# Splitting the operands of a point-wise product, with the low parts of h on VectorE between box sums

## What is computed

```python
x = x + L0(gn(x))   # expert weights mixed by a sparsemax gate, then a 1x1 convolution
x = x + L1(gn(x))   # depthwise 3x3, batch norm, relu, prune; 1x1 convolution, batch norm, relu, prune
x = x + L2(gn(x))   # attention over the 784 pixels with squared, normalised queries and keys
x = x + L3(gn(x))   # 3x3 mean per channel
```

```python
amax = jnp.max(jnp.abs(h), axis=(2, 3), keepdims=True)
h = jnp.where(amax < 4.0, 0, h)                   # whole channels are set to zero
h = conv_general_dilated(h, pw_w, (1, 1), ...)    # the point-wise product, 256 x 256
```

## Time and profile before

| | before |
|---|---|
| median of 3 runs | 1625.71 us (1625.15 to 1627.07) |
| the profiled execution | 1624.92 us, its span 1623.1 us |
| TensorE busy | 1530.0 us, 94% of the span |
| VectorE busy | 1376.0 us, 85% |
| ScalarE busy | 1362.3 us, 84% |
| GpSimd busy | 189.1 us, 12% |
| mean granted TensorE clock | 0.973 of full speed |

### The profile page before, as it was taken

How to read it: one execution, slowest core, us unless ns; L and a number is a source line. 1 busy time by engine, 2 the same in 40 slices (tenths; PEclk the granted TensorE clock), 3 DMA queues, 4 the chain that set the end, 5 groups by cost and what they waited for, 6 DMA issues and landing times. The chain is left out here.

```text
span 1623.1 us, 26428 instructions
## 1 busy us (share of the span) xinstructions
PE 1530.0 (94%) x8190; PEld 1149.4 (71%) x8190; DVE 1376.0 (85%) x2466; ACT 1362.3 (84%) x3496; POOL 189.1 (12%) x142
## 2 busy tenths in 40 slices
PE   4469999999999999999999999999999999999993
PEld 2247777777777777777777777777777777776773
DVE  5877689999888998988889998888999988888446
ACT  3368998988999888899998889999888899987862
POOL 1111011011110101111011111101101111010000
PEclk8689999999999999999999999999999999999996
DMA  4000011000111110011111001111100011000001
GB/s 148 20 20 21 21 40 41 31 29 22 40 40 40 40 40 20 20 40 40 40 40 40 20 20 40 40 40 40 40 27 28 24 40 40 21 21 21 21 20 40
DMA packets 21058, 55.58 MB, mean 34 GB/s; under 512 B 2321, under 2 KB 3345, under 8 KB 21010
## 3 DMA queue, kind: packets, MB, share of 16 engines
q1 hardware_dynamic: 20914, 54.98, 9.6%
q10 hardware_dynamic: 96, 0.00, 0.0%
HBM read 29.29 MB, written 25.69 MB: 34 GB/s over the span
## 5 line engine op out<-in xcount | busy, mean ns | idle before, releaser
L770 DVE SCALAR_TENSOR_TENSOR h<-xpad,dw_sb,h 128x784 f32<-128x784 f32 x512 | 495.9, 1031 | 0.0
L541 PE MATMUL tile_ps<-wqk,xn_parts 128*112 128x512 f32 x1344 | 363.8, 425 | 0.0
L541 PEld LDWEIGHTS tile_ps<-wqk,xn_parts 128*112 128x112 f32 x1344 | 235.3, 175 | 79.6
L583 PE MATMUL tile_ps<-k,xT 112*128 112x256 f32 x896 | 205.2, 388 | 7.7 <-ACT xT L1026 7.7
L583 PEld LDWEIGHTS tile_ps<-k,xT 112*128 112x128 f32 x896 | 174.3, 195 | 40.2 <-issue 8.4
L449 PE MATMUL conv_ps<-h,pw_masked 128*128 128x392 f32 x512 | 180.5, 496 | 5.5 <-issue 5.5
L960 ACT ACTIVATE junk<-x 128x784 bf16<-128x784 f32 x192 | 162.3, 848 | 23.6 <-DVE x L797 15.5
L571 PE MATMUL conv_ps<-x,mixed 128*128 128x392 f32 (+1 forms) x512 | 175.1, 494 | 2.2 <-ACT mixed L994 1.1
L1234 POOL TENSOR_SCALAR pw_masked<-pw_sb,hmask 128x256 f32<-128x256 f32 x64 | 119.1, 1869 | 433.9 <-DVE hmask L778 425.5
L1221 POOL TENSOR_SCALAR xpad<-x,gn_r,gn_s 128x784 f32<-128x784 f32 x64 | 64.4, 1013 | 894.2 <-DVE gn_s L701 894.2
L449 PE MATMUL conv_ps<-xn_parts,w_out 128*128 128x392 f32 x768 | 152.7, 347 | 0.0
(11 more groups left out here) (138 smaller groups left out, 2646.9 us busy)
## 6 DMA issues: line engine op xcount, KB each, us to landing
x<-x SPq DMA_DIRECT2D x32, 784.0 KB, 4.3
out<-x SPq DMA_DIRECT2D x32, 784.0 KB, 3.4
expert_sb<-expert_rows SPq DMA_DIRECT2D x8, 256.0 KB, 5.2
x<-w_qk SPq DMA_DIRECT2D x1, 512.0 KB
x<-w_vT SPq DMA_DIRECT2D x1, 256.0 KB
x<-w_ln SPq DMA_DIRECT2D x1, 256.0 KB
pw_sb<-pw_wT SPq DMA_DIRECT2D x1, 256.0 KB
gmean<-group_mean SPq DMA_DIRECT2D x1, 64.0 KB, 3.8
```

The costliest lines, as they stand in the source:

```text
L541: mm = nc.tensor.matmul(bank, xn2_parts[:, u, i, m * TOK:(m + 1) * TOK], wqk[:, v, i, :], start=False, stop=(i == J - 1 and u == 1))
L583: mm = nc.tensor.matmul(tile_ps[:, KX_BANK, i * C:(i + 1) * C], xT[:, m, half(i)], k2[:, m, :], start=(m == 0), stop=(m == M - 1))
L770: ins = nc.vector.scalar_tensor_tensor(acc, view, scalar, acc, ALU.mult, ALU.add)
```

## The change

The mask is no longer put on the weights but on h, and the product is made of split operands.

- Setup: `pw_parts`, the high and low part of the point-wise weights, is made by VectorE from the loaded weights (a cast and a subtraction, 512 elements each). `mask_weights` is removed.
- GpSimd, `h_high`: for each half, h * mask over 784 elements, written in float32r.
- VectorE, `h_low`: for each half, h * mask - high, over 784 elements. `h_mask` is now two instructions, one for each half, the first of them bound to the first half's sum alone.
- VectorE's order: both masks, box sum 0, low part of half 0, box sum 1, low part of half 1, box sums 2 and 3, `reciprocal_sums`, seven taps, three taps. The reciprocals were behind the seven taps before.
- TensorE: a half of the point-wise product is 12 matmuls on split operands (8 instructions before), and waits for both low parts.
- To make room, `over` has one buffer for all sums and `junk` is shorter, with waits on ScalarE's own earlier instructions.

```diff
             def pointwise(C_, halves):
-                pe.wait_ge(h_ready.sem, h_ready.at(C_))
-                pe.wait_ge(pw_masked_ready.sem, pw_masked_ready.at(C_))
+                pe.wait_ge(h_lo.sem, h_lo.at(C_))
...
-                    conv_tile(j, [(pw_masked[:, i, :], h[:, C_.odd, i, :]) for i in range(J)]).then_inc(pw_mm.sem, 1)
+                    conv_tile(j, by_parts(pw_parts, h_parts)).then_inc(pw_mm.sem, 1)
...
+                parts_of(pw_parts, pw_raw)
                 parts_of(wqk, wqk_raw)
...
+            def h_mask(C_, j):
+
+                dve.wait_ge(h_over_sum.sem, h_over_sum.at(C_, j + 1))
                 if (C_ - 1).active:
+                    dve.wait_ge(h_hi.sem, h_hi.at(C_ - 1))
+                nc.vector.scalar_tensor_tensor(hmask[:, j:j + 1], h_over[:, j:j + 1], ones[:, 0:1], zeros[:], ALU.mult,
+                                               ALU.is_gt).then_inc(hmask_step.sem, 1)
+
+            def h_low(C_, j):
+
+                dve.wait_ge(h_hi.sem, h_hi.at(C_, j + 1))
+                if (C_ - 1).active:
+                    dve.wait_ge(pw_mm.sem, pw_mm.at(C_ - 1))
+                nc.vector.scalar_tensor_tensor(h_parts[:, 1, j, :], h[:, C_.odd, j, :], hmask[:, j:j + 1],
+                                               h_parts[:, 0, j, :].bitcast(F32), ALU.mult,
+                                               ALU.subtract).then_inc(h_lo.sem, 1)
...
                 if C_.active:
-                    h_mask(C_)
+                    h_mask(C_, 0)
+                    h_mask(C_, 1)
                 if F.active:
-                    box_sums(F, range(BOX_STEPS))
+                    box_sums(F, range(1))
+                if C_.active:
+                    h_low(C_, 0)
+                if F.active:
+                    box_sums(F, range(1, 2))
+                if C_.active:
+                    h_low(C_, 1)
+                if F.active:
+                    box_sums(F, range(2, BOX_STEPS))
+                if D.active:
+                    reciprocal_sums(D)
                 if B.active:
                     depthwise(B, slice(3, 10))
-                if D.active:
-                    reciprocal_sums(D)
...
-            def mask_weights(C_):
+            def h_high(C_, j):
 
                 if (C_ - 1).active:
                     pool.wait_ge(pw_mm.sem, pw_mm.at(C_ - 1))
-                pool.wait_ge(w_loaded, LOADED)
-                pool.wait_ge(hmask_step.sem, hmask_step.at(C_))
+                pool.wait_ge(hmask_step.sem, hmask_step.at(C_, j + 1))
                 hold(pool, "pool")
-                for j in range(J):
-                    nc.gpsimd.tensor_scalar(pw_masked[:, j, :], pw_sb[:, j, :], hmask[:, j:j + 1], 0.0, ALU.mult,
-                                            ALU.add).then_inc(pw_masked_ready.sem, 1)
+                nc.gpsimd.tensor_scalar(h_parts[:, 0, j, :], h[:, C_.odd, j, :], hmask[:, j:j + 1], 0.0, ALU.mult,
+                                        ALU.add).then_inc(h_hi.sem, 1)
```

More of the change, by code:

```diff
@@ L131, in build @@
         bn1_sb, bn2_sb = params[:, 4:8, :], params[:, 8:12, :]
-        pw_sb = sb("pw_sb", [P, J, C])
+        pw_parts = sb("pw_parts", [P, 2, J, C], F32R)
         wqk = sb("wqk", [P, 2, J, 2 * C], F32R)
@@ L155, in build @@
         h = sb("h", [P, 2, J, HW])
-        pw_masked = sb("pw_masked", [P, J, C])
+        h_parts = sb("h_parts", [P, 2, J, HW], F32R)
         x2 = sb("x2", [P, 2, J, HW])
@@ L162, in build @@
         k4 = sb("k4", [TOK, M, C])
-        junk = sb("junk", [P, M * C], BF16)
+        junk = sb("junk", [P, J * HW], BF16)
         xT = sb("xT", [TOK, M, C])
@@ L175, in build @@
         wvT_sb, wln_sb = wv_ln[:, 0], wv_ln[:, 1]
+        pw_raw = x3[:, 0].rearrange("p j n -> p (j n)")[:, J * 2 * C:J * 3 * C].rearrange("p (j n) -> p j n", j=J)
         bias_rows = xn2[0:1].rearrange("p j n -> p (j n)")[:, 0:3 * 2 * C].rearrange("p (k n) -> p k n", k=3)
@@ L197, in build @@
         below = sb("below", [P, 2])
-        over = sb("over", [P, 2, J, HW], BF16)
+        over = sb("over", [P, HW], BF16)
         h_over = sb("h_over", [P, J])
@@ L252, in build @@
         h_over_sum = sig("h_over_sum", J)
-        hmask_step = sig("hmask_step")
-        pw_masked_ready = sig("pw_masked_ready", J)
+        hmask_step = sig("hmask_step", J)
+        h_hi = sig("h_hi", J)
+        h_lo = sig("h_lo", J)
         pw_mm = sig("pw_mm", J)
@@ L353, in build @@
             (idn[:], ident),
-            (pw_sb[:], pw_wT.rearrange("(j p) o -> p j o", p=P)),
+            (pw_raw, pw_wT.rearrange("(j p) o -> p j o", p=P)),
         ]
@@ L760, in depthwise @@
                         if (B - 2).active:
-                            dve.wait_ge(pw_mm.sem, pw_mm.at(B - 2))
+                            dve.wait_ge(h_lo.sem, h_lo.at(B - 2))
                     acc = h[:, B.odd, j, :].rearrange("p (h w) -> p h w", w=W)
@@ L771, in depthwise @@
                     ins.then_inc(dw_step[j].sem, 1)
-            def h_mask(C_):
-                dve.wait_ge(h_over_sum.sem, h_over_sum.at(C_))
+            def h_mask(C_, j):
+                dve.wait_ge(h_over_sum.sem, h_over_sum.at(C_, j + 1))
                 if (C_ - 1).active:
-                    dve.wait_ge(pw_masked_ready.sem, pw_masked_ready.at(C_ - 1))
-                nc.vector.tensor_scalar(hmask[:], h_over[:], 0.0, None, ALU.is_gt).then_inc(hmask_step.sem, 1)
+                    dve.wait_ge(h_hi.sem, h_hi.at(C_ - 1))
[8 more added lines that the diff above has]
+                                               ALU.subtract).then_inc(h_lo.sem, 1)
             def make_x2(C_):
@@ L1069, in sum_over_h @@
                     act.wait_ge(hmask_step.sem, hmask_step.at(B - 1))
-                    act.wait_ge(h_over_sum.sem, h_over_sum.at(B - 1, j + 1))
+                    act.wait_ge(y_over_sum.sem, y_over_sum.at(B - 1))
+                if j:
+                    act.wait_ge(h_over_sum.sem, h_over_sum.at(B, j))
                 act.wait_ge(h_ready.sem, h_ready.at(B, j + 1))
-                nc.scalar.activation(over[:, 0, j, :], h[:, B.odd, j, :], ACT.Relu, bias=below[:, 0:1],
+                nc.scalar.activation(over[:], h[:, B.odd, j, :], ACT.Relu, bias=below[:, 0:1],
                                      accum_out=h_over[:, j:j + 1]).then_inc(h_over_sum.sem, 1)
@@ L1078, in sum_over_y @@
                     act.wait_ge(ymask_step.sem, ymask_step.at(C_ - 1))
-                    act.wait_ge(y_over_sum.sem, y_over_sum.at(C_ - 1, j + 1))
+                act.wait_ge(h_over_sum.sem, h_over_sum.at(C_))
+                if j:
+                    act.wait_ge(y_over_sum.sem, y_over_sum.at(C_, j))
                 act.wait_ge(y_ready.sem, y_ready.at(C_, j + 1))
-                nc.scalar.activation(over[:, 1, j, :], x2[:, C_.odd, j, :], ACT.Relu, bias=below[:, 1:2],
+                nc.scalar.activation(over[:], x2[:, C_.odd, j, :], ACT.Relu, bias=below[:, 1:2],
                                      accum_out=y_over[:, j:j + 1]).then_inc(y_over_sum.sem, 1)
@@ L1109, in q_norms @@
                 for m in range(M):
-                    nc.scalar.activation(junk[0:TOK, m * C:(m + 1) * C], q2[:, m, :], ACT.Square,
+                    slot = m % (J * HW // C)
+                    if slot < m:
+                        act.wait_ge(q4_ready.sem, q4_ready.at(D, slot + 1))
+                    nc.scalar.activation(junk[0:TOK, slot * C:(slot + 1) * C], q2[:, m, :], ACT.Square,
                                          scale=qk_rec[:, 0, m:m + 1],
@@ L1241, in step @@
                 if C_.active:
-                    mask_weights(C_)
+                    for j in range(J):
+                        h_high(C_, j)
             run(pool, step)
@@ L1249 @@
 SETUP_BN = SETUP_PARTS + 2
-SETUP_DVE = SETUP_BN + 10 + 2 + 2 + 2
+SETUP_DVE = SETUP_BN + 10 + 2 + 2 + 2 + 2
 SETUP_POOL = 10
```

## The result

The changed kernel takes 1642.08 us (median of 4 runs, 1641.64 to 1643.64) against 1625.86 us before (4 runs, 1625.15 to 1627.07): 1.0101 times the time, 95% interval 1.0088 to 1.0114. It is slower, by about what the prediction said (1640 us). The profiled execution, the longest of the four, took 1643.64 us, its span 1641.8 us.

A forecast was written before the change was run, and what follows sets the result against it. A loop through VectorE, as long as TensorE's, was taken as the bound: step 46.98 + 2.75 - 1.67 - 0.48 = 47.58 us. 1624.92 + 16.2 (27 steps) - 1.6 (ends) = 1639.5, said as 1640 us, range 1624 to 1662.

The forecast's parts named there:

- The shift of the taps, 2.75: On VectorE, the seven taps with the reciprocals ahead of them start 2.75 us later in each step.
- order (b): Box sum 0 runs ahead of GpSimd's first high part; stalls cost VectorE 1.55 us per step; the order taken.
- (a): GpSimd's first high part runs ahead of box sum 0; stalls cost VectorE 1.23 us per step.
- The wait for q_norm: VectorE's wait for q_norm, behind the taps, vanishes: 1.67 us off each step.
- The one for the square root: VectorE's wait for ScalarE's gn_sd shrinks from 0.78 us, taking 0.48 us off each step.
- a rival with a chance of 0.05: TensorE's clock drops behind its 1.6 us wait, 1.76 us per step: 1687 us; chance 0.05.
- the chain that the prediction called fixed: Work from kx_low through attention to the last square of k keeps a fixed distance, 24 us, and absorbs nothing.
- The ends, -1.6: Outside the 27 steps: setup +1.2 us, last two steps and keys_x wait -2.8, together -1.6.
- Full lock: Rival: each high part stops VectorE for 0.99 us, +1.06 us per step: 1652 us; chance 0.12.
- GpSimd slower in the rounded format: Rival: high parts at twice xpad's time give 1693 us, at a third more 1657; chance 0.09.
- Gain and loss cancel: Rival: fixed waits give 0.6 us or reciprocals start by 822.6: 1622 to 1629 us; chance 0.10.
- TensorE alone: Rival: TensorE is the only bound, so each step falls by its 0.8 us: 1603 us; chance 0.14.

The follow-up runs named there:

- experiment 7: Changed kernel with high and low parts on 16 of 784 columns and the reciprocals behind the seven taps, product incomplete: 1617.6 us, ratio 0.9946.
- experiment 4: Changed kernel with the point-wise product in plain float32 of the high parts only, low parts made but not multiplied: 1640.2 us, ratio 1.0091.
- experiment 2: Changed kernel with GpSimd's high parts on 16 of 784 columns, product incomplete: 1646.34 us, ratio 1.0135.
- experiment 9: Changed kernel with only the reciprocals moved behind two of the seven taps, masks late as in the change: 1644.23 us, ratio 1.0107.
- experiment 1: Changed kernel with the reciprocals moved back behind the seven taps: 1733.53 us, ratio 1.0671.
- 8: Changed kernel with the second sum over h and both masks early, reciprocals ahead of all seven taps: 1642.6 us, ratio 1.0106.
- 3: Changed kernel with high parts on 16 columns and the reciprocals behind two of the seven taps, product incomplete: 1602.83 us, ratio 0.986.
- 5: Changed kernel, computing everything, with the second sum over h and both masks early and the reciprocals behind two taps: 1594.71 us, ratio 0.981.
- 6: Kernel before the change with its sum over h and mask early: 1612.03 us, ratio 0.9915.

## Why the prediction was right

**Which loop bounds.** The prediction read from 0.2 us of waiting at kx_parts that a path through VectorE was as long as TensorE's. Shown: experiment 7 gives TensorE 0.9 us and gets 0.23; experiment 4 takes most of its saving back (0.6 us) and the ordinary step stays.

**The shift of the taps, 2.75.** Measured, in the step shown, 24.96 us from kx_low to the reciprocals against 22.29 to the seven taps before (820.44 less the kx_low at 798.15): 2.67. The kx_low of that step:

```profile
798.15 0.69 DVE L879 TENSOR_TENSOR kx_parts<-tile_ps,kx_parts 128x512 fp32r<-128x512 f32 x1 [0.16 <-ACT kx_parts L1127]
```

The prediction had it as the larger of two numbers that lie close together, 2.69 by k and 2.47 to 2.78 by VectorE's own work; both halves are now shown, by experiments 2 and 9. So the size of the stalls hardly mattered here: with none at all the step is the same (experiment 2), and the 2.75 would have come out nearly right with a wrong price. The price had errors. I took order (b), box sum 0 ahead of the first high part. It was (a): the high part started at 871.29, ahead of the second mask. Its price was 1.32, between the 1.23 of (a) and the 1.55 of (b), but it was paid by other instructions than I named: the second mask, for which I had put nothing, pays 0.65, and h_low(0) 0.67. With this price the sum would be 1.54 - 0.31 + 1.32 = 2.55. Most of the last 0.12 lies in the low parts themselves: one between two box sums adds 1.70 + 0.95 - 1.82 = 0.83, where 0.77 was said. How much of it is the wait for k is not separated; experiment 9, where nothing waits for k, is 0.07 shorter.

**What goes behind it.** The wait for q_norm vanished whole, 1.67. The one for the square root went from 0.78 to 0.27, where 0.30 was said. The row of the kernel before:

```profile
844.67 0.20 DVE L699 RECIPROCAL gn_r<-gn_sd 128x8 f32<-128x8 f32 x1 [0.78 <-ACT gn_sd L954]
```

From the step at 798.15 (47.08 us long; 46.98 is the mean of 27) this gives 47.08 + 2.67 - 1.67 - 0.51 = 47.57. Measured 47.47. The last 0.10 is in VectorE's busy time behind the reciprocals and I did not trace it further. Over 27 steps it makes 13.4 us where 16.2 were said.

**The clock.** Here the prediction's own case had nothing, and a rival with a chance of 0.05 had 1.76 us in every step. Neither is what happened: 5 of 27 steps lose 1.6 us, 8.1 in all. This is the largest error of the sum. In such a step the attention weights come late; VectorE in order of time, the low parts of the attention weights:

```profile
813.45 0.88 DVE L858 SCALAR_TENSOR_TENSOR attn_parts<-tile_ps,k_inv,attn_parts 128x256 fp32r<-128x256 f32 x2 [1.88 <-ACT attn_parts L1071]
```

The wait is 1.88 us instead of 0.3, on the chain that the prediction called fixed. Set beside TensorE's rest in an ordinary step, the runs are: 3.4 us in experiment 1 (the granted clock falls in 24 of 27 steps), 0.94 in the change and in experiments 2, 8 and 9 (4 to 6 long steps), 0.5 to 0.6 in 7 and 0.35 in 4 (none), under 0.1 in 3, 5 and 6 (none). Only experiment 4 against the change varies this rest with all other work kept. Why one step in five or six and not each stays open. TensorE's rest was forecast at 1.6 us at kx_parts; it is 0.94 as the trace counts it, most of it one stop earlier at k_norm, and 1.40 against the 46.07 us that TensorE needs when it never waits (experiment 5; forecast 46.0).

**The ends, -1.6.** Measured -2.8: the setup is later by 0.66 at the first kx_low (1.2 forecast), the first step is shorter by 0.81 (not forecast), the last part by 2.66 (2.8 forecast).

Together: 27 steps 2.8 too high, the clock 8.1 too low, the ends 1.2 too high, and the profiled execution took 1643.64 us instead of 1639.5. The mechanism of the ordinary step is the predicted one; that the total came so close is in part luck, for errors of 4 us to one side took half of the 8.1 us to the other away. Of the signs named beforehand three did not come: the wait at kx_parts is 0.4 us and not 1.4 to 1.8, TensorE's busy share of an ordinary step is 98% (46.53 of 47.47) and not under 97%, and h_low(0) starts right behind box sum 0 and not 1 us later; it is stretched while it runs.

**The other rivals.** Full lock: as a mechanism it is what the rows show, in both directions, but its price is not the length of the operations. The second high part lay behind box sum 0 and then held h_low(0), and that cost 0.67 and not 0.92. The Trainium skill's rule named in the prediction says that the two exclude one another for the whole instruction; the order of the rows agrees with it. Why the price is smaller than the length no run shows. GpSimd slower in the rounded format: no, 0.92 us for 784 elements, xpad 0.98. Gain and loss cancel: no, the wait for q_norm and the square root gave 2.18 and nothing ahead of the reciprocals gave way. TensorE alone: no (experiment 7).

## What to carry to other kernels

A small wait of the busiest engine in every step (0.2 us in 47) can tell more than its busy share. Here it meant that a second loop was as long, and 0.9 us of work taken from the first was worth 0.23. When an instruction is moved forward, ask what it waits for at the new place: here three instructions of 0.6 us together, moved over two taps too many, cost 48 us by standing in front of work that was ready (experiments 5 and 8). Where the order allows it, put GpSimd's reads of SBUF beside VectorE instructions that read PSUM; the masks needed only one sum moved ahead of a normalisation on ScalarE for that.

## What the runs showed of the hardware

- A GpSimd operation on SBUF stretches even VectorE's smallest instructions: a mask of one element per partition, read from three SBUF tensors, took 0.85 us while a high part of 0.92 us ran, and 0.23 us with a high part of 16 columns (experiment 2).
- The same two GpSimd operations take 3.91 us beside box sums and 0.93 beside make_x3 (experiment 6).
- TensorE's granted clock fell in some steps and not in others with the same waits in front: 0.8 us for k_norm and 0.3 to 0.4 us for kx_parts in each, a granted clock of 0.53 to 0.61 behind them in 5 steps of 27, 1.00 in the rest. Behind one longer wait of 3.42 us (experiment 1) `mixed_conv` took 7.19 us instead of 5.51.
